# Sliding-window attention, output projection and a LoRA mixture layer on eight cores: scores of two query tiles per round in six PSUM banks, dense work in whole units

## What is computed

```
q, k, v = x @ Wq, x @ Wk, x @ Wv                  # 32 heads of 64
scores = einsum('bnqhd,bnkhd->bhnqk', qb, kc) * scale + bias   # blocks of 512 queries, 1024 keys
scores = where(mask, scores, -1e30)               # 0 <= distance < 512
m = maximum(scores.max(-1), s); p = exp(scores - m)
denom = p.sum(-1) + exp(s - m)                    # s: the head's sink
out = (einsum('bhnqk,bnkhd->bnqhd', p, vc) / denom) @ Wo
x = layernorm(x + out)
x = layernorm(x + x @ weight.T + expert_out)      # 8 LoRA experts of rank 16, top 2 by a router
```

## Time and profile before

| what | us |
|---|---|
| median of 3 runs | 916.93 (916.65 to 919.36) |
| profiled execution, its own time | 914.45 |
| its span on the slowest core (core 6) | 912.9 |
| spans of the eight cores | 908.0 to 912.9 |
| PE busy / DVE busy / ACT busy / POOL busy | 849.6 / 494.7 / 425.7 / 149.1 |
| mean granted TensorE clock of the eight cores | 0.978 to 0.981 |

### The profile page before, as it was taken

One profiled execution on the slowest core, in us unless ns is written; L12 is line 12 of the kernel. 1 busy time (PEld: TensorE's weight loads), 2 busy tenths in 40 slices (PEclk: granted clock), 3 DMA queues, 4 the chain that ended last, 5 costly groups with the idle time before them and its releaser, 6 DMA issues.

```text
span 912.9 us, 18322 instructions; the slowest of 8 cores (908.0 to 912.9 us)
## 1 busy us (share of the span) xinstructions
PE 849.6 (93%) x5880; PEld 466.0 (51%) x5880; DVE 494.7 (54%) x1511; ACT 425.7 (47%) x928; POOL 149.1 (16%) x285
## 2 busy tenths in 40 slices
PE   2499999999999999999999999999599999889996
PEld 0154665555556546556556555554244545444442
DVE  2016756556566565565665655656466437535644
ACT  2026666666666666666666666665200512221000
POOL 6211304301111030030130110026100000000000
PEclk9799999999999999999999999999799999999999
DMA  8999698996795898998988869649949473001312
GB/s 125 149 170 165 89 120 105 166 170 84 99 152 71 124 129 93 130 117 100 113 118 129 114 110 128 131 52 161 201 98 224 86 125 70 1 1 68 155 55 92
DMA packets 127820, 104.73 MB, mean 115 GB/s; under 512 B 81328, under 2 KB 114096, under 8 KB 126192
## 3 DMA queue, kind: packets, MB, share of 16 engines
...
...
## 4 chain that ended last, share of the span: by engine, by line
PE 88%; DMA 6%; POOL 2%; issue 1%; ACT 1%; DVE 1%; DVEq 0%; ACTq 0%; POOLq 0%
PE psP L385 18%; PE psP L356 17%; PE psP L369 12%; PE psS L629 7%; PE psT L469 6%; PE psP L629 5%; PE psP L516 5%; PE psS L516 5%; PE psS L405 5%; PE psP L496 4%; DMA sb<-wv 3%; DMA sb<-xr 2%; POOL sb L200 1%; DMA sb<-wo 1%; PE psT L576 1%
## 5 line engine op out<-in xcount | busy, mean ns | idle before, releaser
L428 DVE CUSTOM_DVE_ANT_0 sb<-psS,sb 128x641 f32<-128x641 f32 (+4 forms) x256 | 171.5, 689 | 116.5 <-PE psS L405 98.0
L445 ACT ACTIVATE sb<-sb 128x641 bf16<-128x641 f32 x256 | 211.9, 833 | 32.0 <-DVE sb L428 16.0
L356 PE MATMUL psP<-sb 128*128 128x512 bf16 x768 | 180.7, 382 | 20.9 <-DMA sb<-xt 20.7
L385 PE MATMUL psP<-sb 128*128 128x256 bf16 x1536 | 180.6, 275 | 10.9 <-DMA sb<-wv 10.7
L485 ACT ACTIVATE sb<-psT 128x640 bf16<-128x640 bf16 x128 | 90.0, 703 | 195.9 <-PE psT L469 195.9
L385 PEld LDWEIGHTS psP<-sb 128*128 128x128 bf16 x1536 | 149.0, 99 | 31.9 <-issue 14.2
L421 DVE CUSTOM_DVE_ANT_0 sb<-psS,sb 128x512 f32<-128x512 f32 (+3 forms) x128 | 62.7, 490 | 129.1 <-PE psS L405 127.3
L356 PEld LDWEIGHTS psP<-sb 128*128 128x128 bf16 x768 | 71.5, 98 | 99.2 <-issue 25.1
L369 PE MATMUL psP<-sb 128*128 128x512 bf16 x512 | 119.4, 383 | 0.0
L457 DVE TENSOR_SCALAR sb<-sb 128x640 bf16<-128x640 bf16 x256 | 88.0, 386 | 13.8
L369 PEld LDWEIGHTS psP<-sb 128*128 128x128 bf16 x512 | 48.6, 99 | 52.2 <-issue 1.4
(11 more groups left out here) (102 smaller groups left out, 699.5 us busy)
## 6 DMA issues: line engine op xcount, KB each, us to landing
...
```

The costliest lines, as they stand in the source:

```text
L356: tok = put("T", lambda t, i=i: t.matmul(bank_ap(bank, [1, 512]), b(WK[pr % 2] + i * 128, [1, 128]), b(XT[blk] + i * 512, [1, 512]), start ...
L385: tok = put("T", lambda t, i=i: t.matmul(bank_ap(bank, [1, 256]), b(XT[blk] + i * 512 + part * 128, [1, 128]), b(WV[g % 2] + i * 256, [1, ...
L428: ttr_last[pr] = ttr_tok[u, hh] = put("V", lambda v: v.tensor_tensor_reduce(out=f(sx + 2 * halo, [1, 641 - halo]), in0=p(psS[hh], 192 + ha ...
L445: e_tok[u, hh] = put("S", lambda s: s.activation(b(pslot(u, hh), [1, 641]), f(SX[hh], [1, 641]), ACT.Exp, bias=f(st + 4 * hh + 2, [1, 1]), ...
```

## The change

The eight PSUM banks are laid out anew: one bank psP for dense work, one for transposes and PV together (psV, and psT is the same bank seen as bfloat16), and three for each of psS0 and psS1. Bank numbers 1 to 6 of `next_bank` are these six, 0 is psP.

The loop goes over rounds of two steps, u and u + 1. `scores` computes both tiles at once, in eight matmuls: 384 and 256 columns of tile u from column 128 of psS on, 256 and 384 of tile u + 1 from column 768 on, so that no matmul crosses a bank. Each matmul waits for what last freed its own bank. Then come `bias_min` and `exponent` for both tiles and heads, `normalise` for both, and two dense *units* of 8192 columns each: one in bank 0, the whole of it, then one in bank 6, the third bank of psS1, with the transposes of both steps in it (four turns in pairs 0 and 15, else two). The last turn comes after the unit's end, unless a PV is due. PV stands at the end of a round.

`Feed` now holds whole units, which are begun in a bank that is named and run by columns or to the end. V tiles come in twos, in one unit of 32 matmuls with one drain of 512 columns. `window_work` queues K of the own block 2 and Q of the own block 1 first, in pair 0 too, where four V tiles stood ahead of them. In pair 0 there are seven units for eight places. In pair 15 PV of n = 0 adds units of one matmul between whole ones.

The sink's column leaves PSUM and the bias buffers: it is written into SX once for each head and pair, ahead of the exponent (L457 after), and the minimum starts from the sink, read per partition from NSK, where it started from a constant. PB has 2 and 7 buffers, before 3 and 6. Transposes now serve the step of their own round, not the one two steps back.

```
+PBN = (2, 7)
+T0, T1 = 128, 768
...
+        self.live = None
...
+    def begin(self, bank=None):
+        self.live = self.work.popleft()(bank) if self.work else None
+
+    def run(self, cols=None):
+        while self.live is not None and (cols is None or cols > 0):
+            done = next(self.live, None)
+            if done is None:
+                self.live = None
+            elif cols is not None:
+                cols -= done
 
...
-    psP = [ctx.enter_context(nc.psum_tensor(f"psP{i}", [128, 512], F32)) for i in range(3)]
-    psT = ctx.enter_context(nc.psum_tensor("psT", [128, 1024], BF16))
-    psS = [ctx.enter_context(nc.psum_tensor(f"psS{i}", [128, 1024], F32)) for i in range(2)]
+    psP = ctx.enter_context(nc.psum_tensor("psP", [128, 512], F32))
+    psV = ctx.enter_context(nc.psum_tensor("psT", [128, 512], F32))
+    psT = psV.bitcast(BF16)
+    psS = [ctx.enter_context(nc.psum_tensor(f"psS{i}", [128, 1536], F32)) for i in range(2)]
...
-    banks = list(psP)
-    bank_free = dict.fromkeys(range(3))
-    bank_ready = collections.deque(range(3))
-
-    def next_bank():
-        k = bank_ready.popleft()
+    banks = [(psP, 0)] + [(psS[i // 3], 512 * (i % 3)) for i in range(6)]
+    bank_free = dict.fromkeys(range(7))
+    bank_ready = collections.deque(range(7))
+
+    def next_bank(k=None):
+        if k is None:
+            k = bank_ready.popleft()
+        else:
+            bank_ready.remove(k)
         return k, banks[k]
...
     def scores(u):
         pr, n, c = steps[u]
-        tile = n * 4 + c
-        for part in range(2):
+        free = [bank_free[k] for k in range(1, 7)]
+        after = [k_tok[pr, n], k_tok[pr, n + 1], q_tok[pr, n]]
+        for which, base, c0, w in ((0, T0, 0, 384), (0, T0, 384, 256),
+                                   (1, T1, 0, 256), (1, T1, 256, 384)):
+            tile = n * 4 + c + which
             for hh in range(2):
-                c0, w = 320 * part, 320
-                s_tok[u, hh] = put("T", lambda t, hh=hh, c0=c0, w=w: t.matmul(
-                    p(psS[hh], 192 + c0, [1, w]),
+                bank = 3 * hh + (base + c0) // 512
+                tok = put("T", lambda t, hh=hh, base=base, c0=c0, w=w, tile=tile: t.matmul(
+                    p(psS[hh], base + c0, [1, w]),
                     b(QT[pr % 2] + tile * 128, [1, 128], row=64 * hh, rows=64),
                     b(KT[pr % 2] + tile * 128 + c0, [1, w], row=64 * hh, rows=64),
                     start=True, stop=True, tile_position=(64 * hh, 0)),
-                    after=[k_tok[pr, n], k_tok[pr, n + 1], q_tok[pr, n], t_pz[hh],
-                           ttr_tok.get((u - 1, hh))], mark=(part == 1))
-        s_last[pr] = s_tok[u, 1]
+                    after=after + [free[bank]], mark=(which == 1))
+                if which == 1:
+                    s_tok[u + (c0 > 0), hh] = tok
+        s_last[pr] = s_tok[u + 1, 1]
...
     def bias_min(u, hh):
         pr, n, c = steps[u]
         st = STA[u % 4]
         sx = SX[hh]
+        h = 2 * pr + hh
+        base = T1 if c % 2 else T0
         halo = (4 - c) * 128 if n == 0 else 0
...
+        init = f(NSK + 2 * h, [1, 1])
         if halo:
...
-            first = put("V", lambda v: v.tensor_tensor_reduce(
-                out=f(sx, [1, halo]), in0=p(psS[hh], 192, [1, halo]),
-                in1=f(HB[pr % 2][hh], [1, halo]), scale=1.0, scalar=HUGE,
+            first = put("V", lambda v, init=init: v.tensor_tensor_reduce(
+                out=f(sx, [1, halo]), in0=p(psS[hh], base, [1, halo]),
+                in1=f(HB[pr % 2][hh], [1, halo]), scale=1.0, scalar=init,
...
-        init = f(st + 4 * hh, [1, 1]) if halo else HUGE
...
+            init = f(st + 4 * hh, [1, 1])
...
+        ttr_last[pr] = ttr_tok[u, hh] = tok
+        for k in ((1, 2) if c % 2 else (0,)):
+            bank_free[1 + 3 * hh + k] = tok
...
-        return PB[hh][u % (3, 6)[hh]]
+        return PB[hh][u % PBN[hh]]
...
+        if n == 0 and c == 0:
+            sink_tok[hh] = put("S", lambda s: s.activation(
+                f(SX[hh] + 2 * 640, [1, 1]), f(NSK + 2 * (2 * pr + hh), [1, 1]), ACT.Copy),
+                after=[t_neg, e_tok.get((u - 1, hh))], mark=True)
         e_tok[u, hh] = put("S", lambda s: s.activation(
...
-            after=[ttr_tok[u, hh], tr_tok.get((u - (3, 6)[hh], hh))], mark=True)
+            after=[ttr_tok[u, hh], sink_tok[hh], tr_tok.get((u - PBN[hh], hh))], mark=True)
...
     def pv(pr, n):
...
-        k, bank = next_bank()
...
-                    p(bank, c0 * 128, [1, (c1 - c0 + 1) * 128], row=64 * hh, rows=64),
+                    p(psV, c0 * 128, [1, (c1 - c0 + 1) * 128], row=64 * hh, rows=64),
...
-                    after=ready + [v_tok[g, n * 4 + kb], bank_free[k]], mark=(kb == 7))
+                    after=ready + [v_tok[g, n * 4 + kb], psT_free[0]], mark=(kb == 7))
...
-        at_tok[pr, n] = release(k, put("V", lambda v: v.tensor_copy(
-            b(AT + pr * 1024 + n * 512, [1, 512]), p(bank, 0, [1, 512])),
-            after=[tok], mark=True))
+        at_tok[pr, n] = psT_free[0] = put("V", lambda v: v.tensor_copy(
+            b(AT + pr * 1024 + n * 512, [1, 512]), p(psV, 0, [1, 512])),
+            after=[tok], mark=True)
...
     def window_work(pr):
+        k_unit(pr, 2)
+        q_unit(pr, 1)
         if pr == 0:
-            v_tiles(0, range(4, 8))
-        k_or_q("k", pr, 2)
-        k_or_q("q", pr, 1)
-        if pr and pr % 2 == 0:
-            v_tiles(pr // 2, range(6, 8))
-        if pr + 1 < NPAIR:
-            if pr:
-                k_or_q("k", pr + 1, 0)
-                k_or_q("k", pr + 1, 1)
-            k_or_q("q", pr + 1, 0)
-        if pr % 2 == 0:
-            v_tiles(pr // 2, range(8, 12))
-        elif pr // 2 + 1 < 8:
-            v_tiles(pr // 2 + 1, range(6))
+            v_units(0, (4, 6))
+        elif pr % 2 == 0:
+            v_units(pr // 2, (6,))
         if pr == 15:
             for t, oc in EARLY:
-                feed.add(("w", t, oc), wo_group(t, oc, 0, NI - 1))
-
-    EARLY = [(0, 0), (1, 0), (2, 0), (0, 1)]
-    LATER = [(3, 0), (1, 1), (2, 1), (3, 1)]
+                wo_unit(t, oc, 0, NI - 1)
+            return
+        if pr:
+            k_unit(pr + 1, 0)
+            k_unit(pr + 1, 1)
+        q_unit(pr + 1, 0)
+        if pr % 2 == 0:
+            v_units(pr // 2, (8, 10))
+        else:
+            v_units(pr // 2 + 1, (0, 2, 4))
...
+    def pv_due(m):
+        if pending_pv and m >= pending_pv[0][0]:
             _, pr, n = pending_pv.popleft()
...
+    U = len(steps) - 2
+    for u in range(0, U + 1, 2):
+        pr, n, c = steps[u]
+        m = u // 2
...
                 load_wo(3, [wk_done[15], wq_done[15], wv_done[7]])
         scores(u)
-        if u > 1:
-            transpose(u - 2, 0)
-            unload(u - 2, 0)
-        bias_min(u, 0)
-        bias_min(u, 1)
-        feed.run(quota * 0.25)
-        exponent(u, 0)
-        feed.run(quota * 0.2)
-        if u > 1 and not by_dma(u - 2, 1):
-            transpose(u - 2, 1)
-            unload(u - 2, 1)
-        exponent(u, 1)
-        if u:
-            normalise(u - 1)
-        if c == 3:
-            pending_pv.append((u + (5 if by_dma(u, 1) else 3), pr, n))
-        pv_due(u)
-        feed.run(quota * 0.55)
+        for w in (u, u + 1):
+            for hh in range(2):
...
-            transpose(u, hh)
-            unload(u, hh)
-            feed.run(4096)
-    pv_due(U + 3)
+        feed.begin(0)
+        feed.run()
+        feed.begin(6)
+        turns = [(w, hh) for w in (u, u + 1) for hh in range(2) if not by_dma(w, hh)]
+        share = {2: (0.45, 0.35, 0.2), 4: (0.2, 0.25, 0.25, 0.2, 0.1)}[len(turns)]
+        if c == 2:
+            pending_pv.append((m + (2 if by_dma(u, 1) else 1), pr, n))
+        late_turn = None
+        for w, hh in turns:
+            feed.run(8192 * share[turns.index((w, hh))])
+            if (w, hh) == turns[-1] and not (pending_pv and m >= pending_pv[0][0]):
+                feed.run()
+            transpose(w, hh)
+            unload(w, hh)
...
+
+    for _ in range(3):
+        feed.begin()
+        feed.run()
+    pv_due(m + 1)
+    U += 1
     late = [pv_last[15], at_tok[15, 1], e_tok[U, 0], e_tok[U, 1]]
```

146 lines of the change are left out of this document (65 added, 81 removed).

## The result

The changed kernel takes 999.43 us (a second run 999.63), before 916.79 (median of 4, 915.96 to 919.36); the ratio is 1.090, 95% interval 1.086 to 1.093. Two more runs, 1023.9 and 1088.5, were in the chip's slower state and are left out, so the median of all four, 1011.7, isn't used. The forecast, 977 with a range to 998, had the sign and the main mechanism, but left out a wait and was 22 us short.

The account below looks back on a forecast made before the run. PE was taken to bound attention at 36.44 us a pair. 914.45 + 47 (pairs 1 to 14) + 11 (pair 0) + 2.5 (pair 15) = 975, and 977 us allowing for the profiled run being 2.5 faster than the median; range 957 to 998.

Parts of the forecast that it names:

- Wait of the second unit for the last pass: Each round's unit 2, in bank 6, waits for the last of four min passes; 60 us over 14 pairs.
- VectorE is the bound: In round 1 (halo, after a PV), VectorE's copy and four passes set the chain before unit 2, 5.97 us.
- PV in the bank of the transposes costs nothing: Sharing one bank adds no wait, as dense matmuls cover the transposes' copy before PV; size zero.
- Savings: Fewer changes of tile shape on PE around scores and PV: 0.9 us a pair, 12.7 us for pairs 1 to 14.
- Start value: Min passes reading a start value per partition take 0.06 us more each; without it, 14 us less in all.
- Pair 0: K of block 2 waits for x, and the last round's transposes stand bare: 47.6 against 36.86 us, +11.
- Pair 15 and the rest: In pair 15, waits mostly hide in VectorE's 12.37 us wait for xr; +2.5 us, bounds -2 and +7.
- Rival, the clock falls: PE's idle time in the 28 halo rounds halves its clock, 48 us more, 1025 us; chance 7%.
- Rival, the chain hides: The four passes end within unit 1, by 4.1 us from the scores, leaving only savings: 913 us; chance 6%.

Follow-up runs that it names:

- e1: The changed kernel with the second unit of each round begun in bank 1 instead of bank 6; 971.9 us, ratio 1.062.
- e7: A reordered two-tile kernel (transposes moved, V's tiles first in pair 0) with the second unit in bank 6 instead of bank 1; 1049.6 us, ratio 1.146.
- e3: The changed kernel with the min passes started from a large constant again instead of the sink read per partition; 989.0 us, ratio 1.081.
- e2: The changed kernel with the transposes placed sooner in two-turn rounds that end with PV; 987.1 us, ratio 1.078.
- e11: The changed kernel with second unit in bank 1, transposes moved, V's tiles first in pair 0, and output weights and residual rows loaded differently; 908.3 us, ratio 0.9886.

## Why the prediction was right or wrong

**Wait of the second unit for the last pass: right.** Forecast 1.9, 1.6, 0.5 and 0.4 us in the four rounds; by the starts in pair 9 it is 1.78, 1.48, 0.61 and 0.27. Rounds 1 and 3, which hold nothing else, were 10.00 and 8.83 against 10.1 and 8.8. e1 and e7 show that the bank is the cause. One part of the chain was read wrongly, at little cost: in the halo rounds "VectorE is the bound" isn't quite so, since the third pass waits for ScalarE's exponent there too (e3).

**"PV in the bank of the transposes costs nothing": the step that failed.** Its reason was that "the last transposes before a PV have their copy done under at least two dense matmuls". I counted matmuls and did not set their 0.43 us against the copy's 1.1, though the same hand-overs stand in my own text for the drain of a unit. It costs 0.58 and 0.46 us by the starts, 1.0 a pair, 14 in all; e2 removed it and gained 12. It is the largest part of the 18 us by which pairs 1 to 14 exceed the forecast (+65.0 by the stages of the two spans, forecast +47). With it, the forecast's own sum gives 991. The rest is pair 0, the loss of clock behind it, and pair 15, below.

**Savings: right in size, 0.9 forecast,** 1.0 in e11 and 1.1 in e1 once the waits are taken out. The forecast's sum itself holds 1.1, not 0.9: four rounds of 4.11 + 4.12 and two of 1.21 more are 35.3, so its +47 is 62 of waiting less 15 saved, not "60 of waiting less 13".

**Start value: right**, 0.06 a pass. It is worth 10 us by e3 where the bound took off 14, since three of the four passes stand in the chain.

**Pair 0: mis-sized, 14.2 us for 11.** The first round took 18.31, forecast 17.1. K's last matmuls started at 73.95 as forecast, but at half clock, as did those up to 79.7: the loss of clock was more than 1.5 us. Rounds 2 and 3 took 11.09 and 11.71, forecast "about 10.4 each". The twenty transposes in its last round stood bare, and behind them the clock fell again, which I had not counted:

```profile
110.00:113.50 3.50, 1.04 (x13) 0.78 (x14) 2.14 (x6) 2.01 (x6) 3.19 (x7) 1.00 0.52 60
113.90:117.40 3.50, 2.34 (x15) 1.21 (x17) 1.26 (x4) 0.77 (x2) 0.71 (x2) 0.50 1.08 85
```

The first round of pair 1 took 12.58 us for it, its like 10.00.

**Pair 15 and the rest: +5.0 for +2.5,** inside its bounds. The loading ahead of pair 0 gave 0.8 more. The hole in which the waits were to hide is there, though smaller (PE waits 4.78 us at 727.68 behind L551).

**Rival, the clock falls: not so in the changed kernel.** The granted clock is 1.00 from 120.70 to 724.80, with PE idle for 1.6 and 1.3 us in a pair, at most 1.9. The rule of the Trainium skill named in the prediction ("TensorE: Matmul & The Clock Gate", A second HAM failure mode) speaks of just such a kernel, with matmuls in groups, short idle gaps and banks in turn; the trace doesn't show the swing here. e7's trace does: with idle times of 2.5 us before the second unit, a stretch of 3.5 us runs at 0.52 of 2.4 GHz once in every two pairs and costs 1.6 us. So the rule is borne out in one kernel of this case and not in the other. In the changed kernel the clock did fall to 0.5 of 2.4 GHz from 69.5, 113.9 and 724.8 us on; PE had worked 1.45, 1.04 and 1.51 us in the rows 66.0 to 69.5, 110.0 to 113.5 and 721.3 to 724.8.

**Rival, the chain hides:** its point, 4.1 us from the scores, holds only for unit 1 in its place. No order tried hid four passes behind one unit; what helped was a bank that doesn't need them.
